# A vision tower on one core: two buffers moved to the front of SBUF, and a new written-out order for every engine

## The chip, the core and the metric

The kernel runs on one core of a Trainium2 chip. Times are device microseconds (us) of one execution. A core has engines that each work through their own list of instructions in order: TensorE (PE; PEld is its weight load), VectorE (DVE), ScalarE (ACT), GpSimd (POOL), and SyncE (SP), which here only issues transfers. Semaphores tie the lists together. 16 DMA engines move data between HBM and the on-chip memory SBUF; TensorE writes to PSUM.

## What is computed

64 images of 12 channels, 224 x 224, pass through one block of a vision transformer. Cut to what matters:

```python
pooled = x.reshape(B, C, 14, 16, 14, 16).sum(axis=(3, 5))         # 16 x 16 patches
h = einsum('bcij,ce->bije', pooled, channel_weights).reshape(B, 196, 192)
h = h + attention(layernorm(h), W_qkv, b_qkv)                     # one head, softmax over 196 keys
h = h + ffn(layernorm(h), w_fc * C0, b_fc * c0b, w_proj * C1, b_proj * c1b)   # tanh GELU, 768 hidden
```

All is float32. The images are 154 MB, the output is 9.6 MB.

## The kernel before, in words

The images are worked through in 16 groups of 4. A group is 3 tiles of 16 image planes; a tile lies in one of the two slots of the ring `xs` (`RING = 2`), with 128 partitions and 7 runs of 896 floats in each. One transfer loads one run of a tile for all partitions (`load`, L403 to L407): 128 rows of 3,584 bytes. SyncE issues the runs of a tile in three chunks of 2, 2 and 3 (`load_chunk`, L409); a chunk waits until VectorE has summed the chunk that lay in the same place two tiles earlier (L414).

VectorE sums each chunk over its patches (`reduce_chunk`, L464, the instruction at L474), nine chunks a group, and does a few small steps of each group between them: `variance1`, `maxima` (L490), `context`, `variance2`.

TensorE takes a group's sums (`sum_rows`, L702) when all nine are there, and then goes through the chain of the attention: `turn_phat`, `apply_a`, `scores` (L730), `turn_maxima`, `turned_scores`, `weigh`, `turn_context`, `turn_u`, `apply_g2`, `turn_uhat` (L796), with ScalarE's copies out of PSUM, VectorE's steps and GpSimd's scalings between them. Then come `hidden` in three pairs, each followed by ScalarE's GELU and rounding to a high part and GpSimd's low part (`low_part`), and `project` in 24 parts of 6 matmuls (L823), on top of `residual`. ScalarE copies the results out of PSUM (`take_out`, L1012, the copy at L1016), and SyncE stores them in two transfers for each group (`send`, L418).

What each engine does next is written out by hand. `PE_ORDER`, `ACT_ORDER`, `DVE_ORDER`, `POOL_ORDER` and `SP_ORDER` (L72 to L200) give for each kind of work one number for each of the 16 groups. Group m's work stands at step `PERIOD * m` plus that number, `PERIOD` being 254, and each engine's list is made by walking through the steps. Only the order that results reaches the chip; what waits for what is in the semaphores. TensorE, for one, works on several groups at a time: behind `sum_rows` of the last group in its list there still stand all 24 parts of `project` of groups 13, 14 and 15, and some of group 12.

Buffers are laid out in SBUF in the order in which they are declared, each start rounded up to 32 bytes. `xs` is declared at L279, behind 25 buffers of constants and weights, and starts at byte 49,952 of each partition. That is 32 bytes past a multiple of 64, and 32 past a multiple of 256. All 14 rows of a partition in it start 32 bytes past a multiple of 64 too, since a row is 56 x 64 bytes. `out_sb` (L296), from which the results are stored in rows of 1,536 bytes, starts at 215,648, also 32 past a multiple of 64.

Of the kernel before, what the change touches and what calls it, by code (L numbers as in the profile page):

```python
# [17 lines left out]
EMBED = 192  # L18
# [9 lines left out]
HALF = TOKENS // 2  # L28
# [9 lines left out]
RUNS = GRID // 2  # L38
RUN = 4 * SIDE
# [31 lines left out]
STEPS = 4907  # L71
PE_ORDER = {  # L72
    "sum_rows": (443, 399, 379, 379, 370, 383, 371, 360, 348, 336, 325, 312, 318, 310, 312, 330),
    "turn_phat": (518, 475, 471, 450, 443, 470, 471, 459, 448, 421, 410, 397, 395, 366, 396, 397),
    "apply_a": (531, 487, 494, 473, 466, 495, 495, 483, 472, 444, 432, 420, 419, 400, 414, 410),
    "scores": (545, 624, 528, 543, 506, 528, 514, 502, 490, 479, 467, 455, 443, 422, 451, 430),
    "turn_maxima": (601, 693, 643, 596, 573, 579, 568, 556, 544, 533, 520, 498, 497, 488, 485, 464),
    "turned_scores": (615, 707, 657, 610, 588, 595, 583, 571, 560, 548, 536, 513, 512, 503, 513, 480),
    "weigh": (644, 739, 695, 646, 619, 631, 619, 608, 596, 584, 572, 544, 543, 549, 559, 516),
    "turn_context": (663, 780, 732, 675, 643, 658, 646, 634, 623, 611, 598, 587, 570, 572, 590, 542),  # L80
    "turn_u": (701, 813, 753, 706, 671, 707, 695, 684, 672, 660, 648, 636, 592, 626, 607, 570),
    "apply_g2": (714, 826, 788, 735, 699, 728, 717, 705, 693, 682, 669, 658, 610, 641, 632, 589),
    "residual": (
        (720, 836, 1053, 1046, 1031, 1019, 1007, 996, 984, 972, 960, 960, 928, 924, 893, 828),
        (970, 1174, 1187, 1157, 1145, 1134, 1122, 1110, 1098, 1086, 1080, 1065, 1032, 1042, 997, 913),
    ),
    "turn_uhat": (763, 882, 835, 808, 765, 802, 790, 779, 767, 738, 732, 726, 685, 714, 693, 635),
    "hidden": (
# [3 lines left out]
    ),  # L92
    "project": (
# [27 lines left out]
    "load_exp": (360, 626, 481, 544, 502, 500, 525, 513, 501, 490, 478, 466, 454, 450, 446, 432),  # L121
    "copy_p_tok": (455, 409, 396, 389, 383, 411, 393, 381, 369, 358, 346, 334, 347, 322, 337, 340),
    "copy_phat": (525, 482, 483, 465, 455, 489, 479, 467, 456, 436, 424, 412, 408, 377, 404, 405),
    "copy_b": (540, 497, 503, 484, 478, 523, 509, 497, 485, 465, 454, 441, 430, 415, 435, 421),
    "copy_maxima": (610, 702, 651, 604, 582, 588, 576, 565, 553, 541, 529, 506, 506, 497, 493, 473),
    "exponentials": (628, 720, 670, 623, 602, 608, 596, 585, 573, 561, 549, 526, 525, 516, 527, 493),
    "load_gelu": (642, 938, 898, 870, 881, 869, 858, 846, 834, 822, 795, 799, 785, 795, 761, 677),
    "copy_context": (657, 752, 716, 664, 632, 649, 638, 626, 614, 603, 590, 560, 560, 563, 574, 532),
    "copy_u": (709, 820, 782, 720, 693, 722, 710, 699, 687, 675, 663, 651, 602, 634, 621, 582),
    "keep_u": (713, 824, 793, 735, 729, 749, 738, 726, 701, 690, 677, 678, 606, 638, 633, 593),  # L130
    "copy_uhat": (770, 889, 842, 815, 790, 810, 798, 786, 775, 747, 740, 733, 694, 723, 701, 656),
    "gelu": (
# [6 lines left out]
    ),  # L139
    "round_high": (  # L140
# [6 lines left out]
    ),  # L147
    "take_out": (
# [4 lines left out]
    ),  # L153
}
DVE_ORDER = {
# [39 lines left out]
    ),  # L195
    "send": (
        (1066, 1272, 1285, 1255, 1244, 1231, 1220, 1208, 1196, 1180, 1176, 1163, 1130, 1140, 1095, 1011),
        (1188, 1405, 1398, 1379, 1367, 1355, 1343, 1332, 1319, 1308, 1312, 1276, 1275, 1243, 1180, 1096),
    ),
}  # L200
SETUP_AT = {
# [954 lines left out]
```

## Time and profile before

| | us |
|---|---|
| runs shown | 493.0, 492.98, 492.1 (median 492.98) |
| the profiled execution | 492.97 |
| its span, first to last instruction | 491.2 |
| TensorE busy | 424.0 (86% of the span) |
| VectorE busy | 381.6 (78%) |
| ScalarE busy | 286.9 (58%) |
| GpSimd busy | 255.5 (52%) |
| DMA share while images are loaded | 1.03 |
| last reduction of the last group ends | 423.7 |
| last matmul ends | 487.5 |

The profile is one execution taken by the hardware profiler. A row of windows gives for a stretch of time how long each engine was busy in it and how many instructions it ran. The chain of waits is followed back from the last instruction: each piece is what released the next. Where rows name a line such as L602, that is a helper which emits every matmul; such rows are told apart by their operands. Matmuls overlap in the pipeline, so their durations add up to more than the busy time; the spacing of their starts is what one costs in a row of them. TensorE's granted clock has two levels, 2.4 and 1.2 GHz; the windows give its mean as a share of the higher.

### The profile page before, as it was taken

How to read it: one execution, taken by the hardware profiler on the slowest of the kernel's cores; microseconds unless marked ns; L12 is line 12 of the kernel's file. 1: busy time of each engine (PE TensorE's matmuls, PEld its weight loads, DVE VectorE, ACT ScalarE, POOL GpSimd, SP SyncE). 2: the span in 40 equal slices, each digit the busy share in tenths (PEclk: the TensorE clock that was granted, in tenths of full speed). 3: DMA queues.
4: the chain of work that ended last, by engine and by line, in shares of the span. 5: the costliest groups of instructions: out<-in, count | busy, mean ns of one | idle time of the engine just before them, and what ended most of it. 6: DMA issues, size and time to landing. Idle time of an engine off the chain costs nothing.

```text
span 491.2 us, 10938 instructions
## 1 busy us (share of the span) xinstructions
PE 424.0 (86%) x4558; PEld 360.5 (73%) x4558; DVE 381.6 (78%) x272; ACT 286.9 (58%) x478; POOL 255.5 (52%) x194
## 2 busy tenths in 40 slices
PE   5966466976989999899998979899999989999996
PEld 4533234864778888688887968887878878888996
DVE  1789998999899998899989898989998887610000
ACT  1022036514877856658585949485858566877821
POOL 1023225503757491738374938375745665576840
PEclk9996555995699999989999999899999989999999
DMA  8999999999999999999999999999999997101101
GB/s 256 360 403 405 401 402 402 402 403 405 402 403 402 404 402 404 400 398 404 397 404 399 400 397 399 400 396 399 402 402 400 397 399 308 34 26 35 41 26 50
DMA packets 56661, 166.65 MB, mean 339 GB/s; under 512 B 5972, under 2 KB 13030, under 8 KB 56612
## 3 DMA queue, kind: packets, MB, share of 16 engines
q1 hardware_dynamic: 56612, 165.95, 87.7%
q8 instruction: 36, 0.59, 0.5%
q14 instruction: 13, 0.11, 0.1%
HBM read 156.29 MB, written 9.63 MB: 338 GB/s over the span
## 4 chain that ended last, share of the span: by engine, by line
DMA 49%; PE 23%; DVE 18%; SPq 5%; issue 3%; ACT 1%; DVEq 0%
DMA xs<-x 49%; PE ps L602 22%; DVE pooled L474 17%; SPq L406 5%; DMA cw_sb<-cw 0%; DVE phat_tok L492 0%; ACT out_sb L1016 0%; PE ps L799 0%; ACT probs L905 0%; DVEq L469 0%; PE ps L779 0%; DVE prod L483 0%; PE ps L786 0%; ACT qkt L903 0%; SPq L425 0%
## 5 line engine op out<-in xcount | busy, mean ns | idle before, releaser
L474 DVE TENSOR_REDUCE pooled<-xs 128x28 f32<-128x1792 f32 x144 | 329.5, 2324 | 29.0 <-DMA xs<-x 28.3
L1114 POOL TENSOR_TENSOR h_lo<-h_f,h_hi 128x784 fp32r<-128x784 f32 x96 | 177.1, 1871 | 76.7 <-ACT h_hi L1010 76.7
L602 PE MATMUL ps<-w_hi,h_hi 128*98 128x192 f32 x768 | 207.1, 270 | 1.1 <-POOL h_lo L1114 1.0
L602 PE MATMUL ps<-w_lo,h_hi 128*98 128x192 f32 x768 | 196.5, 256 | 0.0
L602 PE MATMUL ps<-w_hi,h_lo 128*98 128x192 f32 x768 | 196.2, 255 | 0.0
L602 PEld LDWEIGHTS ps<-w_hi,h_hi 128*98 128x98 f32 x768 | 128.4, 167 | 16.7 <-issue 14.5
L602 PEld LDWEIGHTS ps<-w_lo,h_hi 128*98 128x98 f32 x768 | 128.9, 168 | 0.0
L602 PEld LDWEIGHTS ps<-w_hi,h_lo 128*98 128x98 f32 x768 | 128.5, 167 | 0.0
L1001 ACT ACTIVATE h_f<-ps 128x784 f32<-128x784 f32 x96 | 75.8, 827 | 21.4 <-PE ps L602 20.4
L1010 ACT CAST h_hi<-h_f 128x784 fp32r<-128x784 f32 x96 | 78.4, 855 | 0.0
L1091 POOL TENSOR_TENSOR inv<-var,minus_half 98x8 f32<-98x8 f32 x16 | 26.2, 1640 | 77.4 <-DVE var L488 77.4
L602 PE MATMUL ps<-rows_sb,f_rows 32*128 32x196 f32 x768 | 50.6, 382 | 6.0 <-ACT h_f L1001 3.7
L1016 ACT COPY out_sb<-ps 98x384 f32<-98x384 f32 x64 | 30.2, 477 | 30.8 <-PE ps L602 30.6
L602 PEld LDWEIGHTS ps<-rows_sb,f_rows 32*128 32x128 f32 x768 | 34.6, 203 | 15.3 <-issue 5.9
L1105 POOL TENSOR_TENSOR inv<-var,minus_half 98x8 f32<-98x8 f32 x16 | 26.2, 1640 | 28.2 <-DVE var L513 28.2
L960 ACT ACTIVATE probs<-ps 98x1568 f32<-98x1568 f32 x16 | 23.7, 1481 | 23.5 <-PE ps L602 23.5
L492 DVE TENSOR_REDUCE phat_tok<-ps 98x8 f32<-98x1568 f32 x16 | 28.5, 1784 | 6.5 <-PE ps L602 6.5
L602 PE MATMUL ps<-rows_sb 32*98 32x196 f32 x512 | 31.6, 363 | 1.8 <-ACT rows_sb L953 1.2
L602 PE MATMUL ps<-resid,rows_sb 32*98 32x192 f32 x256 | 27.9, 336 | 2.5 <-ACT out_sb L1016 2.5
L953 ACT COPY rows_sb<-ps 128x196 f32<-128x196 f32 x16 | 5.2, 323 | 36.8 <-PE ps L756 36.7
L602 PEld LDWEIGHTS ps<-rows_sb 32*98 32x98 f32 x512 | 20.4, 169 | 6.4 <-ACT rows_sb L953 2.0
L602 PEld LDWEIGHTS ps<-resid,rows_sb 32*98 32x98 f32 x256 | 20.1, 163 | 5.3 <-ACT out_sb L1016 3.7
(119 smaller groups left out, 340.2 us busy)
## 6 DMA issues: line engine op xcount, KB each, us to landing
xs<-x SPq DMA_DIRECT2D x336, 448.0 KB, 12.5
out<-out_sb SPq DMA_DIRECT2D x32, 294.0 KB
rows_sb<-wfc SPq DMA_DIRECT2D x1, 576.0 KB, 5.7
out_sb<-wproj SPq DMA_DIRECT2D x1, 576.0 KB, 9.4
h_f<-wqkv SPq DMA_DIRECT2D x1, 432.0 KB
cf<-const_full SPq DMA_DIRECT2D x1, 264.0 KB, 2.8
h_f<-const_paired SPq DMA_DIRECT2D x1, 153.0 KB, 3.3
cr<-const_rows SPq DMA_DIRECT2D x1, 83.2 KB
```

The costliest lines, as they stand in the source:

```text
L406: sp.dma_start(xs[:, tile % RING, i], x_runs[2 * PLANES * tile:2 * PLANES * (tile + 1), :, i]).then_inc(x_landed[tile % RING][i], 16)
L474: dve.tensor_reduce(pooled[:, n % 2, t, GRID * first:GRID * end].rearrange("p (i j) -> p i j", j=GRID), runs, AX.XY, ALU.add).then_inc(red ...
L492: dve.tensor_reduce(phat_tok[:, m % 2, :, :, NEG].rearrange("p h b -> p b h"), ps[0:HALF, 0:GROUP, 0:2 * TOKENS].rearrange("p b (h k) -> p ...
L602: return pe.matmul(o, a, b, start=start, stop=stop, skip_group_check=shared)
L953: act.copy(phat_neg, ps[:, MB, 0:TOKENS]).then_inc(phat_neg_ready, 1)
L960: act.activation(probs[:], ps[0:HALF, 0:GROUP, 0:2 * TOKENS], ACT.Exp).then_inc(probs_ready, 1)
L1001: act.activation(h_f32[:, t].rearrange("p (b n) -> p b n", b=GROUP), ps[:, 0:GROUP, TOKENS * (t % 2):TOKENS * (t % 2 + 1)], ACT.Gelu_apprx ...
L1010: act.copy(h_hi[:, m % 2, t], h_f32[:, t]).then_inc(h_hi_ready, 1)
L1016: act.copy(out_sb[:, b // 2, b % 2], ps[0:HALF, OB + b % 2, 0:2 * EMBED]).then_inc(out_ready, 1)
L1091: pool.tensor_tensor(inv1[:], var1[:], minus_half[:], ALU.pow).then_inc(inv1_ready, 1)
L1105: pool.tensor_tensor(inv2[:], var2[:], minus_half[:], ALU.pow).then_inc(inv2_ready, 1)
L1114: pool.tensor_tensor(h_lo[:, m % 2, t], h_f32[:, t], h_hi[:, m % 2, t].bitcast(F32), ALU.subtract).then_inc(h_lo_ready, 1)
```

## The change

`xs` and `out_sb` are declared first of all buffers. `xs` then starts at byte 16,512 (258 x 64, and 128 past a multiple of 256), `out_sb` at 66,688 (1,042 x 64, and 128 past a multiple of 256). Every other buffer moves by a multiple of 256 bytes (by 56,320 those ahead of `xs` before, by 6,144 those behind it), so its place within 64 or 256 bytes stays. All five tables are replaced; the work itself, its tiles, semaphores and waits stay as they are. Of the tables the diff below shows the rows of which the next sections speak; the columns are groups 0 to 15.

```diff
-STEPS = 4907
+STEPS = 4901
 PE_ORDER = {
-    "sum_rows": (443, 399, 379, 379, 370, 383, 371, 360, 348, 336, 325, 312, 318, 310, 312, 330),
+    "sum_rows": (443, 399, 379, 361, 374, 370, 363, 346, 339, 330, 316, 307, 298, 293, 287, 275),
...
-    "turn_context": (663, 780, 732, 675, 643, 658, 646, 634, 623, 611, 598, 587, 570, 572, 590, 542),
+    "turn_context": (663, 766, 694, 657, 658, 687, 669, 653, 644, 639, 630, 621, 602, 555, 527, 516),
...
     "residual": (
-        (720, 836, 1053, 1046, 1031, 1019, 1007, 996, 984, 972, 960, 960, 928, 924, 893, 828),
-        (970, 1174, 1187, 1157, 1145, 1134, 1122, 1110, 1098, 1086, 1080, 1065, 1032, 1042, 997, 913),
+        (720, 824, 1046, 1034, 1009, 991, 975, 966, 961, 953, 944, 940, 918, 910, 867, 802),
+        (970, 1171, 1173, 1149, 1132, 1093, 1083, 1093, 1084, 1066, 1046, 1054, 1043, 1015, 971, 887),
     ),
...
     "project": (
-        (857, 1025, 1065, 1066, 1051, 1039, 1027, 1016, 1007, 995, 983, 969, 937, 933, 902, 854),
-        (894, 1063, 1086, 1055, 1040, 1028, 1017, 1005, 996, 981, 969, 974, 948, 967, 933, 837),
-        (931, 1127, 1116, 1097, 1100, 1088, 1077, 1051, 1038, 1035, 1029, 1020, 1000, 1002, 964, 875),
-        (868, 1046, 1122, 1071, 1060, 1048, 1036, 1024, 1012, 1000, 989, 985, 942, 956, 913, 859),
-        (899, 1073, 1111, 1092, 1080, 1069, 1057, 1045, 1033, 1030, 1009, 1006, 976, 997, 949, 864),
-        (937, 1138, 1153, 1117, 1105, 1094, 1082, 1070, 1058, 1046, 1035, 1031, 1005, 1013, 970, 886),
-        (873, 1036, 1070, 1082, 1070, 1059, 1047, 1035, 1023, 1016, 999, 1000, 971, 951, 907, 870),
-        (910, 1079, 1105, 1060, 1045, 1034, 1022, 1010, 1001, 990, 974, 980, 987, 982, 944, 843),
-        (942, 1143, 1158, 1123, 1111, 1099, 1087, 1076, 1063, 1060, 1040, 1036, 1011, 1007, 975, 881),
-        (862, 1031, 1076, 1112, 1086, 1074, 1062, 1065, 1053, 1041, 1015, 1026, 982, 961, 918, 891),
-        (905, 1068, 1091, 1077, 1065, 1053, 1042, 1030, 1017, 1010, 994, 991, 953, 977, 938, 848),
-        (952, 1149, 1164, 1128, 1116, 1105, 1093, 1081, 1069, 1066, 1045, 1042, 1016, 1018, 981, 897),
-        (1012, 1208, 1221, 1168, 1156, 1144, 1133, 1121, 1109, 1097, 1089, 1082, 1042, 1081, 1017, 933),
-        (982, 1258, 1262, 1193, 1182, 1170, 1158, 1147, 1134, 1122, 1123, 1107, 1123, 1092, 1023, 939),
-        (1029, 1263, 1268, 1210, 1198, 1186, 1174, 1163, 1150, 1139, 1142, 1124, 1129, 1102, 1028, 966),
-        (1007, 1252, 1226, 1204, 1192, 1181, 1169, 1157, 1145, 1133, 1137, 1118, 1118, 1107, 1012, 960),
-        (988, 1190, 1251, 1179, 1167, 1155, 1144, 1132, 1119, 1108, 1104, 1102, 1109, 1052, 1039, 922),
-        (1045, 1277, 1276, 1241, 1229, 1217, 1211, 1199, 1187, 1170, 1168, 1138, 1134, 1123, 1060, 971),
-        (1023, 1217, 1235, 1246, 1234, 1223, 1216, 1205, 1192, 1175, 1173, 1143, 1076, 1113, 1050, 949),
-        (1051, 1185, 1202, 1173, 1162, 1150, 1138, 1126, 1114, 1102, 1095, 1097, 1081, 1063, 1006, 944),
-        (1061, 1222, 1246, 1252, 1240, 1228, 1222, 1210, 1198, 1186, 1179, 1153, 1087, 1118, 1055, 955),
-        (1018, 1247, 1241, 1199, 1187, 1175, 1164, 1152, 1140, 1128, 1131, 1113, 1047, 1058, 1033, 976),
-        (1056, 1283, 1197, 1228, 1216, 1204, 1196, 1184, 1172, 1160, 1157, 1129, 1062, 1087, 1044, 928),
-        (1070, 1288, 1282, 1262, 1251, 1239, 1227, 1216, 1203, 1191, 1196, 1162, 1153, 1129, 1066, 982),
+        (857, 1021, 1060, 1049, 1031, 1014, 984, 975, 984, 963, 967, 954, 939, 919, 876, 816),
+        (894, 1060, 1055, 1043, 1026, 1009, 995, 986, 978, 973, 953, 949, 944, 930, 892, 811),
+        (931, 1120, 1101, 1089, 1072, 1055, 1046, 1041, 1030, 1025, 1014, 1009, 995, 965, 938, 827),
+        (868, 1038, 1066, 1068, 1051, 1030, 1015, 1006, 1000, 993, 984, 974, 950, 924, 881, 860),
+        (899, 1076, 1071, 1074, 1056, 1036, 1020, 1011, 1005, 999, 989, 979, 970, 981, 912, 843),
+        (946, 1125, 1106, 1094, 1077, 1061, 1052, 1047, 1035, 1030, 1019, 1014, 1006, 987, 944, 865),
+        (873, 1032, 1081, 1063, 1042, 1025, 1010, 1000, 994, 988, 978, 969, 990, 945, 923, 822),
+        (910, 1065, 1117, 1109, 1092, 1050, 1035, 1025, 1019, 1013, 1003, 995, 976, 960, 917, 849),
+        (937, 1131, 1146, 1114, 1097, 1071, 1061, 1061, 1050, 1040, 1025, 1020, 1001, 976, 949, 854),
+        (862, 1027, 1086, 1054, 1037, 1020, 990, 981, 989, 968, 973, 960, 960, 970, 887, 833),
+        (905, 1070, 1111, 1079, 1062, 1045, 1026, 1017, 1014, 1004, 998, 989, 955, 940, 907, 838),
+        (952, 1151, 1151, 1120, 1102, 1076, 1067, 1067, 1055, 1045, 1030, 1025, 1020, 992, 954, 870),
+        (979, 1198, 1217, 1158, 1141, 1107, 1098, 1110, 1101, 1075, 1061, 1065, 1066, 1031, 1007, 896),
+        (1033, 1227, 1211, 1169, 1152, 1127, 1118, 1121, 1112, 1095, 1090, 1076, 1088, 1070, 1012, 939),
+        (1038, 1264, 1241, 1184, 1167, 1141, 1132, 1136, 1127, 1109, 1095, 1081, 1094, 1086, 1023, 945),
+        (1015, 1233, 1182, 1189, 1172, 1156, 1146, 1141, 1132, 1124, 1112, 1099, 1060, 1037, 996, 901),
+        (1028, 1253, 1193, 1164, 1146, 1122, 1112, 1116, 1107, 1090, 1084, 1071, 1055, 1051, 1018, 918),
+        (1044, 1269, 1257, 1197, 1180, 1163, 1154, 1149, 1140, 1135, 1117, 1105, 1135, 1097, 1029, 950),
+        (984, 1180, 1188, 1234, 1217, 1201, 1192, 1187, 1174, 1169, 1165, 1143, 1104, 1026, 980, 928),
+        (990, 1238, 1226, 1226, 1208, 1192, 1183, 1178, 1165, 1161, 1159, 1135, 1099, 1075, 991, 912),
+        (1022, 1258, 1235, 1240, 1223, 1206, 1197, 1192, 1180, 1175, 1170, 1149, 1124, 1092, 1034, 934),
+        (1009, 1211, 1262, 1220, 1203, 1178, 1168, 1172, 1160, 1146, 1131, 1116, 1119, 1042, 1002, 907),
+        (1004, 1216, 1246, 1202, 1185, 1169, 1159, 1154, 1145, 1140, 1126, 1110, 1141, 1081, 985, 923),
+        (1058, 1274, 1268, 1245, 1228, 1212, 1203, 1197, 1188, 1180, 1175, 1154, 1146, 1102, 1039, 955),
     ),
...
 DVE_ORDER = {
     "reduce": (
-        (101, 162, 140, 114, 123, 114, 105, 96, 87, 78, 69, 60, 55, 53, 54, 55),
+        (100, 162, 140, 114, 123, 114, 105, 96, 87, 78, 69, 60, 51, 42, 33, 24),
...
-        (387, 365, 338, 347, 338, 329, 320, 311, 302, 293, 285, 279, 278, 279, 280, 297),
+        (387, 365, 338, 329, 338, 329, 320, 311, 302, 293, 285, 276, 267, 258, 249, 240),
     ),
...
 SP_ORDER = {
     "load": (
-        (98, 110, 103, 94, 73, 64, 60, 51, 42, 33, 24, 15, 10, 1, 0, 8),
+        (118, 130, 123, 114, 93, 84, 80, 71, 57, 48, 44, 35, 21, 12, 3, 0),
...
     ),
     "send": (
-        (1066, 1272, 1285, 1255, 1244, 1231, 1220, 1208, 1196, 1180, 1176, 1163, 1130, 1140, 1095, 1011),
-        (1188, 1405, 1398, 1379, 1367, 1355, 1343, 1332, 1319, 1308, 1312, 1276, 1275, 1243, 1180, 1096),
+        (1086, 1289, 1291, 1267, 1250, 1211, 1201, 1205, 1193, 1180, 1164, 1172, 1156, 1126, 1089, 1005),
+        (1196, 1418, 1406, 1381, 1363, 1347, 1337, 1333, 1324, 1316, 1312, 1290, 1282, 1237, 1174, 1090),
     ),
...
...
             return ctx.enter_context(nc.semaphore(name))
 
 
+        xs = sb("xs", [128, RING, RUNS, RUN])
+        out_sb = sb("out_sb", [HALF, 2, 2, 2 * EMBED])
+
+
         cf = sb("cf", [128, FULL])
         cr = sb("cr", [CHANNELS, ROWS])
         cw_sb = sb("cw_sb", [CHANNELS, EMBED])
...
         table_out = sb("table_out", [1, 1])
 
 
-        xs = sb("xs", [128, RING, RUNS, RUN])
         pooled = sb("pooled", [128, 2, TILES, HALF])
         u_tok = sb("u_tok", [HALF, 2, 2, GROUP, Q])
         prod1 = sb("prod1", [HALF, 2 * GROUP, CHANNELS + 1])
...
         h_f32 = sb("h_f32", [128, H_SLOTS, GROUP_TOKENS])
         h_hi = sb("h_hi", [128, 2, HT, GROUP_TOKENS], F32R)
         h_lo = sb("h_lo", [128, 2, HT, GROUP_TOKENS], F32R)
-        out_sb = sb("out_sb", [HALF, 2, 2, 2 * EMBED])
 
         phat_rows, phat_neg, b_rows, context_rows, u_rows, uhat_rows = (rows_sb[:, i] for i in range(6))
         u_kept = [rows_sb[:, 6], rows_sb[:, 7]]
```

## Rows read from the trace of the kernel before

**Rows 1.** The page: busy time by engine, and moved GB/s in 40 equal slices.

```profile
...
PE 424.0 (86%) x4558; PEld 360.5 (73%) x4558; DVE 381.6 (78%) x272; ACT 286.9 (58%) x478; POOL 255.5 (52%) x194
...
GB/s 256 360 403 405 401 402 402 402 403 405 402 403 402 404 402 404 400 398 404 397 404 399 400 397 399 400 396 399 402 402 400 397 399 308 34 26 35 41 26 50
```

**Rows 2.** The page: chain that ended last, shares by line.

```profile
...
DMA xs<-x 49%; PE ps L602 22%; DVE pooled L474 17%; SPq L406 5%; DMA cw_sb<-cw 0%; DVE phat_tok L492 0%; ACT out_sb L1016 0%; PE ps L799 0%; ACT probs L905 0%; DVEq L469 0%; PE ps L779 0%; DVE prod L483 0%; PE ps L786 0%; ACT qkt L903 0%; SPq L425 0%
```

**Rows 3.** Chain from 396 us on: start us, length us, what ran.

```profile
...
453.70 17.70 PE ps L602 x208
...
480.02 7.53 PE ps L602 x80
```

**Rows 4.** Windows: length, busy us (and count) per engine, granted clock, DMA share, GB/s.

```profile
...
core 0: us, PE busy (x) PEld busy (x) DVE busy (x) ACT busy (x) POOL busy (x), PEclk, DMA share, GB/s
162.70:423.70 261.00, 242.19 (x2879) 213.95 (x2878) 235.72 (x160) 180.11 (x299) 152.72 (x111) 0.98 1.00 388
423.70:487.60 63.90, 62.28 (x728) 56.27 (x726) 4.65 (x12) 37.88 (x64) 39.21 (x25) 1.00 0.10 30
36.00:162.70 126.70, 93.86 (x867) 72.20 (x868) 119.86 (x80) 62.14 (x104) 58.65 (x42) 0.73 1.03 403
```

**Rows 5.** Timeline of VectorE about the last reductions of groups 5 and 15: start, length.

```profile
...
157.83 4.87 DVE L474 TENSOR_REDUCE pooled<-xs 128x28 f32<-128x1792 f32 x2
...
414.08 9.66 DVE L474 TENSOR_REDUCE pooled<-xs 128x42 f32<-128x2688 f32 x4
```

**Rows 6.** Waits, 162.7 to 423.7 us, VectorE's (and SyncE's queue, 95 to 406).

```profile
...
DVE pooled L474 <- DMA xs<-x: 21.0, 27, 1.7
DVE phat_tok L492 <- PE ps L602: 2.1, 1, 2.1
...
SPq L406 <- DVE pooled L474: 89.5, 64, 3.4
SPq L420 <- ACT out_sb L1016: 3.0, 4, 2.1
```

**Rows 7.** VectorE's instructions by form, whole span: busy us, mean ns, idle before.

```profile
...
L474 DVE TENSOR_REDUCE pooled<-xs 128x28 f32<-128x1792 f32 x96 | 190.6, 2011 | 3.7 <-DMA xs<-x 3.3
L474 DVE TENSOR_REDUCE pooled<-xs 128x42 f32<-128x2688 f32 x48 | 141.6, 2950 | 25.3 <-DMA xs<-x 24.9
```

**Rows 8.** TensorE's waits, 162.7 to 423.7 us: total, times, longest.

```profile
...
PE ps L799 <- POOL uhat_tok L1107: 11.0, 7, 3.3
PE ps L602 <- DVE pooled L474: 3.1, 3, 1.5
```

**Rows 9.** Windows by rate, columns as in group 4.

```profile
...
12.00:15.00 3.00, 3.00 (x16) 3.00 (x15) 2.77 (x2) 0.02 (x1) 0.00 (x0) 1.00 1.03 408
...
162.70:406.00 243.30, 224.49 (x2662) 198.65 (x2661) 220.12 (x152) 167.11 (x278) 146.25 (x106) 0.98 1.03 400
```

**Rows 10.** Timeline of TensorE: one residual and three matmuls of a project part.

```profile
...
408.24 0.89 PE L602 MATMUL ps<-resid,rows_sb 32*98 32x192 f32 x8
409.06 0.33 PE L602 MATMUL ps<-w_hi,h_hi 128*98 128x192 f32 x1
409.23 0.25 PE L602 MATMUL ps<-w_lo,h_hi 128*98 128x192 f32 x1
409.32 0.25 PE L602 MATMUL ps<-w_hi,h_lo 128*98 128x192 f32 x1
409.41 0.26 PE L602 MATMUL ps<-w_hi,h_hi 128*98 128x192 f32 x1
```

**Rows 11.** The page: transfers, KB of one, us from issue to landing.

```profile
...
xs<-x SPq DMA_DIRECT2D x336, 448.0 KB, 12.5
out<-out_sb SPq DMA_DIRECT2D x32, 294.0 KB
```

**Rows 12.** Timeline at the end: last copy out of PSUM, issue of last store.

```profile
...
487.57 0.48 ACT L1016 COPY out_sb<-ps 98x384 f32<-98x384 f32 x1 [0.58 <-PE ps L602]
488.07 0.32 SPq L420 DMA_DIRECT2D out<-out_sb  x1
```

More of the change, by code:

```diff
@@ L70 @@
 PERIOD = 254
-STEPS = 4907
+STEPS = 4901
 PE_ORDER = {
-    "sum_rows": (443, 399, 379, 379, 370, 383, 371, 360, 348, 336, 325, 312, 318, 310, 312, 330),
[L74 to L79, printed above, removed]
-    "turn_context": (663, 780, 732, 675, 643, 658, 646, 634, 623, 611, 598, 587, 570, 572, 590, 542),
-    "turn_u": (701, 813, 753, 706, 671, 707, 695, 684, 672, 660, 648, 636, 592, 626, 607, 570),
-    "apply_g2": (714, 826, 788, 735, 699, 728, 717, 705, 693, 682, 669, 658, 610, 641, 632, 589),
+    "sum_rows": (443, 399, 379, 361, 374, 370, 363, 346, 339, 330, 316, 307, 298, 293, 287, 275),
+    "turn_phat": (518, 475, 458, 449, 441, 470, 455, 438, 412, 403, 407, 423, 370, 361, 378, 323),
+    "apply_a": (531, 487, 541, 471, 460, 489, 493, 476, 462, 453, 445, 440, 424, 388, 400, 368),
+    "scores": (545, 624, 556, 537, 518, 511, 509, 492, 493, 483, 461, 471, 450, 419, 422, 389),
+    "turn_maxima": (601, 688, 633, 589, 568, 576, 559, 558, 549, 529, 518, 527, 501, 477, 458, 427),
+    "turned_scores": (615, 703, 646, 603, 584, 592, 575, 574, 564, 544, 533, 543, 527, 492, 473, 443),
+    "weigh": (644, 741, 676, 634, 629, 632, 615, 624, 615, 594, 585, 593, 567, 523, 504, 489),
+    "turn_context": (663, 766, 694, 657, 658, 687, 669, 653, 644, 639, 630, 621, 602, 555, 527, 516),
+    "turn_u": (701, 801, 733, 677, 691, 723, 706, 690, 680, 675, 663, 658, 629, 588, 544, 540),
+    "apply_g2": (714, 819, 750, 699, 714, 743, 725, 709, 700, 695, 690, 685, 647, 622, 563, 558),
@@ L83 @@
     "residual": (
-        (720, 836, 1053, 1046, 1031, 1019, 1007, 996, 984, 972, 960, 960, 928, 924, 893, 828),
-        (970, 1174, 1187, 1157, 1145, 1134, 1122, 1110, 1098, 1086, 1080, 1065, 1032, 1042, 997, 913),
+        (720, 824, 1046, 1034, 1009, 991, 975, 966, 961, 953, 944, 940, 918, 910, 867, 802),
+        (970, 1171, 1173, 1149, 1132, 1093, 1083, 1093, 1084, 1066, 1046, 1054, 1043, 1015, 971, 887),
     ),
-    "turn_uhat": (763, 882, 835, 808, 765, 802, 790, 779, 767, 738, 732, 726, 685, 714, 693, 635),
+    "turn_uhat": (763, 864, 828, 781, 805, 794, 787, 777, 768, 757, 755, 740, 711, 672, 652, 609),
@@ L120 @@
 ACT_ORDER = {
[L121 to L131, printed above, removed]
-    "gelu": (
[6 rows of a table removed]
+    "load_exp": (360, 626, 480, 535, 511, 488, 507, 490, 481, 472, 459, 447, 445, 430, 419, 413),
+    "copy_p_tok": (455, 409, 396, 371, 391, 417, 385, 368, 362, 353, 338, 326, 331, 316, 301, 285),
+    "copy_phat": (525, 482, 477, 460, 451, 480, 471, 454, 457, 447, 423, 434, 414, 378, 395, 359),
+    "copy_b": (540, 497, 551, 488, 476, 503, 504, 487, 478, 469, 456, 462, 434, 398, 416, 379),
+    "copy_maxima": (610, 697, 641, 598, 577, 585, 568, 567, 558, 538, 526, 536, 510, 485, 466, 436),
+    "exponentials": (628, 716, 660, 616, 597, 605, 588, 587, 577, 557, 546, 556, 541, 505, 486, 456),
+    "load_gelu": (642, 928, 884, 865, 873, 856, 855, 846, 831, 819, 824, 809, 774, 755, 724, 643),
+    "copy_context": (657, 754, 689, 648, 647, 649, 632, 643, 633, 610, 599, 612, 588, 544, 520, 502),
+    "copy_u": (709, 808, 745, 686, 706, 737, 719, 699, 690, 689, 684, 680, 640, 608, 558, 547),
+    "keep_u": (713, 812, 820, 717, 737, 753, 735, 727, 717, 705, 696, 714, 699, 644, 569, 551),
+    "copy_uhat": (770, 871, 836, 790, 813, 801, 795, 785, 776, 764, 763, 748, 719, 696, 662, 621),
+    "gelu": (
[6 rows of a table added]
     ),
     "round_high": (
[6 rows of a table removed]
[6 rows of a table added]
     ),
     "take_out": (
[4 rows of a table removed]
[4 rows of a table added]
     ),
@@ L156 @@
     "reduce": (
[9 rows of a table removed]
-    ),
-    "variance1": (486, 435, 426, 417, 408, 434, 425, 416, 407, 363, 354, 349, 353, 334, 349, 347),
-    "maxima": (581, 662, 556, 574, 545, 556, 527, 518, 509, 501, 495, 474, 475, 436, 464, 443),
-    "context": (694, 804, 746, 697, 653, 673, 664, 656, 652, 647, 608, 601, 582, 609, 596, 549),
-    "variance2": (729, 848, 801, 772, 713, 754, 745, 736, 727, 692, 684, 685, 643, 651, 640, 598),
[9 rows of a table added]
+    ),
+    "variance1": (486, 435, 426, 417, 408, 434, 390, 381, 372, 363, 354, 375, 336, 327, 324, 290),
+    "maxima": (581, 662, 613, 554, 545, 536, 527, 518, 509, 501, 492, 503, 474, 445, 436, 403),
+    "context": (694, 784, 726, 667, 682, 699, 690, 661, 652, 663, 654, 645, 616, 572, 533, 522),
+    "variance2": (729, 830, 781, 722, 733, 754, 745, 736, 727, 718, 709, 700, 662, 633, 572, 566),
 }
 POOL_ORDER = {
-    "scale_p": (493, 442, 433, 424, 415, 441, 444, 432, 421, 371, 362, 356, 367, 341, 368, 370),
-    "scale_u": (738, 857, 810, 781, 736, 776, 765, 753, 740, 713, 707, 700, 655, 682, 666, 607),
+    "scale_p": (493, 442, 433, 424, 415, 444, 397, 389, 380, 371, 362, 395, 344, 335, 351, 297),
+    "scale_u": (738, 839, 804, 748, 776, 767, 758, 749, 740, 731, 727, 713, 686, 646, 611, 576),
     "low_part": (
[6 rows of a table removed]
[6 rows of a table added]
     ),
```

80 rows, old and new, of tables (ACT_ORDER, DVE_ORDER, PE_ORDER, POOL_ORDER) are left out of this document.

## Prediction

> **What bounds the kernel now.** I read the page first. TensorE is busy for 86% of the span and VectorE for 78%, and the moved GB/s stand at 396 to 405 from the third slice of the span to the thirty-third and drop to some 30 behind it [rows 1]. So there are two stretches with different limits: images arrive until about 420 us, and then something runs for 70 us without them. The chain of waits says the same: 49% of the span is images landing, 17% VectorE's sums over them, 5% SyncE issuing the next load, and 22% TensorE [rows 2], and from 396 us on nearly every long piece is TensorE [rows 3].
>
> Next I cut the span where the images end. The last reduction of group 5 ends at 157.83 + 4.87 = 162.7 us, that of group 15 at 414.08 + 9.66 = 423.7 us [rows 5]. That is 261.0 us for ten groups, 26.1 us a group. In this stretch VectorE is busy for 235.7 us, TensorE for 242.2, and the DMA share is 1.00, 1.03 until the loads run out [rows 4, 9]. All three are near full. Which ends last is seen in the waits: VectorE sat idle before 27 reductions for 21.0 us until images landed, and only 3.0 us until TensorE was done [rows 6]. So the images set the pace, but by little: without the wait for them VectorE would need 240 us for the ten groups (24.0 a group), and TensorE's busy time is 24.2 a group. Over the whole span VectorE waits 28.2 us for images [rows 7].
>
> Behind 423.7 us TensorE is busy for 62.3 of 63.9 us [rows 4]: this stretch is the work that stands in TensorE's list behind the last group's `sum_rows`, and it starts when that group's images are summed. Then follow the last copy at 487.57 us, the last store's issue at 488.07 [rows 12], and its landing. Profiled, the execution took 492.97 us, 1.8 more than the span and practically the median of the runs (492.98); I make the sum against 492.97.
>
> **Part 1, the buffers' places.** It removes and adds no instruction. What it can change is the time of one row's landing. A group brings 21 transfers of 448 KB and two stores of 294 KB [rows 11], 10.24 MB; at the 400 GB/s of the stretch [rows 9] that is 25.6 us of the 26.1. With the engines' share at 1.03 there is no gap to close, so a faster group needs faster rows. No row of this trace shows a row of images landing at another offset, so I bound the group's time. The slow end is 26.1 us, if the place makes no difference. I set no loss: each row keeps its length and its 3,584 bytes, the source stays, and the start only goes from 32 past a multiple of 64 to a multiple. The fast end is set by the engines behind the loads: VectorE's 24.0 and TensorE's 24.2. The highest rate that a window shows is 408 GB/s [rows 9], in the first images, before VectorE had work for more than one chunk; 400/408 of 26.1 would be 25.6, but that rate was reached at the old place, and says nothing of the new. Nothing here lies nearer to one end than to the other, so I take the middle of 24.0 and 26.1, 25.05 us. Ten groups then end at 162.7 + 250.5 = 413.2 us: **10.5 us earlier**.
>
> The page "DMA: Bandwidth & Descriptors" of the Trainium skill, section "Where 436 GB/s comes from", puts the ceiling of the 16 ports at 435 GB/s; as an estimate, 400/435 of 26.1 is 24.0 us a group, so the ceiling would not bind ahead of the two engines. The same page, section "How a descriptor splits into AXI transactions", speaks against the change: what costs is a start off a multiple of 256 bytes on the side that is read. That side is HBM here and does not move, and 16,512 is off 256 too; by this rule the images would land no faster, which is the first rival below.
>
> Before 162.7 us the images' share of VectorE's waits is 28.2 - 21.0 = 7.2 us, and TensorE is far from full there: 93.9 of 126.7 us at a mean granted clock of 0.73 [rows 4]. Work there hangs on latencies and on setup, so I count nothing, with a bound of 3 us gained. `out_sb`'s new place touches 32 stores, of which only the last is on the path, issue to landing about 3 us: nothing, with a bound of 0.3 either way.
>
> **Part 2, the new orders.** Of TensorE's list I count what stands behind the last group's `sum_rows`, as that work cannot start before group 15's images are summed. Steps behind 254 x 15 + 330 = 4140 before, 4085 after: groups 13 to 15 have all 24 project parts there in both. Of group 12 (254 x 12 = 3048) it is the parts later than 1092 before, 6 of them, and those later than 1037 after, 12 of them. So six parts more. Matmuls of a part start 0.09 us apart [rows 10]; 6 x 6 x 0.09 = 3.2 us. The second `residual` of group 12 (1043) also falls behind now, 0.8 us [rows 10], and `turn_context` of group 14 (527) moves ahead, two matmuls, 0.2 us. Sum +3.8 us. TensorE's idle of 63.9 - 62.3 = 1.6 us could take up part of it, so 2.2 to 3.8; I take **+3.0 us**. If the images come no faster, nothing covers it. These parts are taken out of the time before `sum_rows`, where TensorE must have room: it idles 18.8 us in 162.7 to 423.7, of which 11.0 is `turn_uhat` waiting for GpSimd and 3.1 the wait for reductions [rows 8]. The first hangs on `variance2`, which stands in VectorE's list behind reductions that wait for images, so these waits shrink with them. 10.5 - 3.0 = 7.5 us of the 18.8 have to go; that leaves more than 1 us a group for latencies.
>
> VectorE's, ScalarE's and GpSimd's lists hold the same instructions. SyncE's loads move 2 us later against its stores. A store that waits for `out_ready` holds up the loads behind it; in 95 to 406 us this cost 3.0 us of SyncE's time in four waits, against 89.5 us of waiting for reductions [rows 6], and a load is issued 12.5 us before it lands [rows 11], so such a wait is covered. Nothing, with a bound of 1 us lost: the cover goes if a store waits longer than those 12.5 us.
>
> **Sum.** 492.97 - 10.5 + 3.0 = 485.5 us. The end follows group 15's images one for one, since TensorE is full behind them.
>
> **Rivals.** First, the place makes no difference. Then the group stays at 26.1 us, the last images are summed at 423.7 as before, and six more parts and a residual stand behind them: 492.97 + 2.2 to 3.8 = 495.2 to 496.8, or from 493.5 if the earlier stages that the new order puts ahead shorten the path too. For it: nothing in the trace shows an effect of the place. By the rule of the Trainium skill above it is the case to expect. Against it: with engines at 1.03 and a steady 403 GB/s [rows 4], the pace is that of one row, which is what the place could touch. This is the slower side, and its price decides it: images must end over 3.0 us earlier, that is below 25.8 us a group, or the new order loses.
>
> Second, a small effect, 25.5 to 25.8 us a group: images 3 to 6 us earlier, the order 3 us later, 490 to 493.
>
> Third, images come as fast as the engines take them. At 24.5 us a group, the last are summed 16 us earlier, and 3.0 us of it go back: 480. TensorE would have to lose 13 of its 18.8 us idle, which the wait for GpSimd alone hardly allows; with 10 to 13 gained, 480 to 483.
>
> Fourth, TensorE's list waits where it did not before, since it was laid out for other arrival times: `project` parts late, a store held up, `out_sb` not free. Some 2 to 4 us on the forecast, 488 to 490, or on the first rival, 497 to 499.
>
> **Chances.** My forecast with its own range, 483 to 489 us: 0.45. Engines take over, 480 to 483: 0.13. Small effect, 489 to 493.5: 0.13, of which 0.05 lies within 0.2% (1.0 us, about what a measurement of this kernel can tell from no change). No effect of the place, 493.5 to 496.8: 0.25, of which 0.03 within 0.2%. A badly fitting order, slower: 0.04. So faster 0.45 + 0.13 + 0.08 = 0.66, same 0.08, slower 0.26. The range goes from 481, which leaves out 0.05 below, to 496, which leaves out about 0.12 above.
>
> **What would show it.** Right: 415 to 420 GB/s in the slices in which now 400 stand; VectorE's wait for images well under 21 us; the last reduction ending at 410 to 416 us; about 67 us from there to the last copy (63.9 now), with TensorE full. Wrong: slices at 400 and a last reduction at 423 (first rival), VectorE's reductions back to back with a DMA share under 1 (third), or TensorE idle behind the last reduction (fourth).

## The result, and the profile after

The changed kernel takes 489.63 us (median), the kernel before 492.99 beside it: ratio 0.9927, 95% interval 0.9905 to 0.9948, 3.4 us less. The forecast was 485.5, 7.5 us less. The direction was right and the time lies in the range, but only 3.4 us of the 7.5 came. The profiled execution took 489.43 us over a span of 487.6.

The moved GB/s of the changed kernel in 40 slices, and its chain of waits by line (of [rows 1] and [rows 2]):

```profile
...
GB/s 245 345 406 407 405 406 404 406 408 409 406 406 407 408 409 406 410 403 407 408 404 406 410 404 406 407 405 407 405 407 407 406 404 273 28 26 40 37 26 51
...
```

```profile
...
DMA xs<-x 48%; PE ps L604 21%; DVE pooled L476 18%; SPq L408 4%; DVE phat_tok L494 1%; DMA cw_sb<-cw 0%; POOL h_lo L1116 0%; POOL inv L1107 0%; ACT out_sb L1018 0%; PE ps L781 0%; DVE prod L485 0%; PE ps L758 0%; ACT probs L907 0%; DVE var L490 0%; PE ps L801 0%
...
```

The slices stand at 403 to 410, where 396 to 405 stood. I had asked for 415 to 420. The chain has the same shape as before. Next the windows, cut where the last reductions of groups 5 and 15 end (of [rows 4]):

```profile
...
core 0: us, PE busy (x) PEld busy (x) DVE busy (x) ACT busy (x) POOL busy (x), PEclk, DMA share, GB/s
163.80:416.70 252.90, 236.21 (x2824) 206.02 (x2824) 234.93 (x161) 177.04 (x295) 152.41 (x110) 0.99 1.00 397
416.70:484.10 67.40, 66.14 (x776) 59.99 (x768) 4.71 (x11) 41.42 (x67) 39.43 (x25) 1.00 0.11 33
...
```

VectorE's timeline of the changed kernel about these two reductions (start and length in us, line, operation and tiles; of [rows 5]):

```profile
...
158.95 4.87 DVE L476 TENSOR_REDUCE pooled<-xs 128x28 f32<-128x1792 f32 x2
...
408.05 1.78 DVE L494 TENSOR_REDUCE phat_tok<-ps 98x8 f32<-98x1568 f32 x1
409.75 6.91 DVE L476 TENSOR_REDUCE pooled<-xs 128x28 f32<-128x1792 f32 x3
...
```

Group 5 ends at 158.95 + 4.87 = 163.8 us, 1.1 us later than before. Group 15 ends at 409.75 + 6.91 = 416.7 us, 7.0 us earlier. In between a group takes 25.3 us (26.1 before). The window from 416.7 us to just behind the start of the last copy out of PSUM (484.0) has 67.4 us (63.9 before), with TensorE busy for 66.1 of it and 776 matmuls in place of 728. So images end 7.0 us earlier, and 3.5 us of that are given back behind them; the other half is the gain.

VectorE's waits of the changed kernel in the first of these windows (us in total, times, longest; of [rows 6]):

```profile
...
DVE pooled L476 <- DMA xs<-x: 16.0, 18, 1.9
...
```

TensorE's in the same window (of [rows 8]):

```profile
...
PE ps L801 <- POOL uhat_tok L1109: 6.4, 7, 2.3
PE ps L604 <- DVE pooled L476: 6.0, 8, 1.2
...
```

VectorE still waits 16.0 us for images (21.0 before), and TensorE's wait for GpSimd's `uhat_tok` fell from 11.0 to 6.4 us. The images still set the pace; they only set a slightly faster one.

### The profile page after: what moved, and what is told of

Read it like the earlier page. It is cut to its first block, busy times and chain, and to the rows that moved or that the text cites. A ratio compares the mean times of both kernels' runs of the same rounds, so it can differ in the third digit from the quotient of the medians.

```text
span 487.6 us, 10938 instructions
## 1 busy us (share of the span) xinstructions
PE 426.1 (87%) x4558; PEld 359.6 (74%) x4558; DVE 380.3 (78%) x272; ACT 287.5 (59%) x478; POOL 255.3 (52%) x194
## 4 chain that ended last, share of the span: by engine, by line
DMA 48%; PE 22%; DVE 20%; SPq 5%; issue 3%; ACT 1%; POOL 1%; DVEq 0%
DMA xs<-x 48%; PE ps L604 21%; DVE pooled L476 18%; SPq L408 4%; DVE phat_tok L494 1%; DMA cw_sb<-cw 0%; POOL h_lo L1116 0%; POOL inv L1107 0%; ACT out_sb L1018 0%; PE ps L781 0%; DVE prod L485 0%; PE ps L758 0%; ACT probs L907 0%; DVE var L490 0%; PE ps L801 0%
## 5 line engine op out<-in xcount | busy, mean ns | idle before, releaser
L1003 ACT ACTIVATE h_f<-ps 128x784 f32<-128x784 f32 x96 | 75.7, 827 | 22.9 <-PE ps L604 22.6
L1012 ACT CAST h_hi<-h_f 128x784 fp32r<-128x784 f32 x96 | 79.8, 854 | 0.0
L494 DVE TENSOR_REDUCE phat_tok<-ps 98x8 f32<-98x1568 f32 x16 | 28.5, 1784 | 9.4 <-PE ps L604 9.4
L992 ACT COPY rows_sb<-ps 128x196 f32<-128x196 f32 x16 | 8.4, 522 | 34.5 <-PE ps L801 34.5
```

Of the source, the lines that this page charges most:

```text
L494: dve.tensor_reduce(phat_tok[:, m % 2, :, :, NEG].rearrange("p h b -> p b h"), ps[0:HALF, 0:GROUP, 0:2 * TOKENS].rearrange("p b (h k) -> p ...
L992: act.copy(uhat_rows.rearrange("p (h n) -> p n h", h=2), ps[:, MB, 0:TOKENS].rearrange("p (n h) -> p n h", h=2)).then_inc(uhat_rows_ready, 1)
L1003: act.activation(h_f32[:, t].rearrange("p (b n) -> p b n", b=GROUP), ps[:, 0:GROUP, TOKENS * (t % 2):TOKENS * (t % 2 + 1)], ACT.Gelu_apprx ...
L1012: act.copy(h_hi[:, m % 2, t], h_f32[:, t]).then_inc(h_hi_ready, 1)
```

## The experiments

The theory: the images' rows land faster at the new place, and the new order costs time behind the last image. The rival: the place does nothing, and the pace comes from the order in which SyncE issues transfers. A further question: why the gain in rate was so small.

### Each part alone

The tables of before with the new places:

```diff
 (after)
-PE_ORDER, ACT_ORDER, DVE_ORDER, POOL_ORDER, SP_ORDER, STEPS of after
+those of before
```

> The five tables of before, xs and out_sb declared first. Theory 1 (the place makes the images' rows land faster, the new order costs time behind the last image): 405 to 407 GB/s while images load, about 25.3 us a group, the last reduction ends at 416 to 418 us, 63.9 us from there to the last copy as before, time 485.5 to 487.5. Rival (the place does nothing, the images' pace comes from the order in which SyncE issues loads and stores): 400 to 403 GB/s, last reduction at 423 to 424, 492 to 494.

The tables of after with the old places:

```diff
 (before)
-PE_ORDER, ACT_ORDER, DVE_ORDER, POOL_ORDER, SP_ORDER, STEPS of before
+those of after
```

> The five tables of after, xs and out_sb declared where they stood before. Theory 1: 400 to 403 GB/s, 26.1 us a group, last reduction at 423 to 425 us, 67.3 us from there to the last copy, time 495 to 498. Rival (order alone): 406 GB/s, last reduction at 417, time 489 to 490.

Windows of the first (columns as in the windows above): its rates are those of after.

```profile
...
24.00:60.00 36.00, 19.59 (x77) 11.74 (x76) 32.08 (x20) 7.36 (x16) 11.53 (x6) 0.69 1.03 406
165.00:400.00 235.00, 219.10 (x2598) 194.09 (x2597) 216.55 (x150) 163.75 (x272) 142.54 (x102) 0.98 1.03 406
...
```

Windows of the second: its rates are those of before.

```profile
...
24.00:60.00 36.00, 21.00 (x77) 12.65 (x75) 32.14 (x20) 7.36 (x15) 11.54 (x6) 0.80 1.03 403
165.00:400.00 235.00, 215.61 (x2564) 188.29 (x2563) 214.18 (x146) 161.85 (x268) 138.73 (x100) 0.99 1.03 400
...
```

Place alone: 487.89 us, ratio 0.9893 (0.9863 to 0.9922). Order alone: 495.04 us, ratio 1.0042 (1.0020 to 1.0063). The rival falls, since the rate follows the place. The whole gain is the place's. Yet the place alone gave less than I had expected of it before the run: its last reduction ends at 419.6 us where 416 to 418 were expected, at the expected rate of 406 GB/s. The order costs 2 us at the old place, and at the new one the median is 1.7 us above that of the place alone (there the two intervals still overlap a little). In one table, from the profiled executions, one for each kernel (group pace and stretches from VectorE's timeline and the last copy's start); such an execution can lie a microsecond off its kernel's median, as that of e1_place_only does (488.93 us):

| kernel | tables | `xs` past a multiple of 256 | GB/s, 24 to 60 / 165 to 400 us | group 5 ends | us a group, 5 to 15 | group 15 ends | from there to last copy |
|---|---|---|---|---|---|---|---|
| before | before | 32 | 403 / 400 | 162.7 | 26.1 | 423.7 | 63.9 |
| e2_order_only | after | 32 | 403 / 400 | 163.9 | 25.8 | 422.1 | 67.9 |
| e1_place_only | before | 128 | 406 / 406 | 162.1 | 25.75 | 419.6 | 63.8 |
| after | after | 128 | 406 / 406 | 163.8 | 25.3 | 416.7 | 67.3 |
| e5_256_old_order | before | 0 | 417 / 411 | 161.9 | 25.2 | 413.5 | 63.8 |
| e3_xs_256 | after | 0 | 417 / 411 | 160.8 | 24.95 | 410.3 | 67.1 |

The last column shows the order's cost: 3.3 to 4.0 us at each place. The column before it shows a gain of the order that I had not counted: group 15 ends 1.6 to 3.2 us earlier with the new tables. VectorE's timeline in e1_place_only shows from where:

```profile
...
408.27 1.79 DVE L494 TENSOR_REDUCE phat_tok<-ps 98x8 f32<-98x1568 f32 x1 [2.09 <-PE ps L604]
409.97 9.66 DVE L476 TENSOR_REDUCE pooled<-xs 128x42 f32<-128x2688 f32 x4
```

With the old tables VectorE stands idle for 2.09 us before `maxima` (L494) of group 14, because TensorE's `scores` are not there, and four reductions of group 15 stand behind it. In after the same `maxima` at 408.05 has no wait ahead of it and three reductions follow (the timeline above). Over the ten groups VectorE's waits for TensorE in e1_place_only (162.1 to 419.6 us) are these two lines:

```profile
...
DVE phat_tok L494 <- PE ps L604: 4.1, 2, 2.1
DVE prod L510 <- PE ps L604: 2.1, 2, 1.5
...
```

That is 6.2 us, against 0.5 in after (2.9 in before, none in e2_order_only). So part of the pace of after is the order's: images at 406 GB/s with the old tables gave 25.75 us a group.

### Another place for the images, and for the output

```diff
 (after)
+        sb("pad", [128, 32])           # 128 bytes: xs and out_sb at multiples of 256
         xs = sb("xs", [128, RING, RUNS, RUN])
         out_sb = sb("out_sb", [HALF, 2, 2, 2 * EMBED])
+        sb("pad2", [128, 32])
```

> As after, with 128 bytes of padding ahead of xs, so that xs and out_sb start at a multiple of 256 (a further 128 bytes behind them keep the other buffers' places). If 64 bytes are what counts: as after, 406 GB/s with images alone, 407 with stores beside them, time 489 to 490.5. If the pieces of a row are cut at multiples of 256 bytes on the landing side too, a row has 14 pieces in place of 15: rate up once more, 410 to 415 GB/s, last reduction at 411 to 414 us, time 484 to 487.

Windows of e3_xs_256, and VectorE's wait for images in it (160 to 410.4 us):

```profile
...
24.00:60.00 36.00, 22.01 (x89) 13.45 (x91) 33.14 (x20) 7.68 (x16) 11.54 (x6) 0.81 1.03 417
165.00:400.00 235.00, 221.61 (x2645) 193.92 (x2637) 220.51 (x154) 167.13 (x277) 147.59 (x108) 0.99 1.03 411
...
```

```profile
...
DVE pooled L478 <- DMA xs<-x: 13.3, 16, 2.1
...
```

482.62 us, ratio 0.9780 (0.9749 to 0.9811): 417 GB/s with images alone, 411 with stores beside them, 24.95 us a group. The rate and the time are better than either branch expected. It is about the pace that I had forecast for the change (25.05), 128 bytes further on; the images end at 410.3, within the forecast's 410 to 416. One row of 3,584 bytes takes a DMA engine 140.1 ns on average between 24 and 60 us here, 144.1 in after and 145.4 in before (from the DMA packets in the traces), so the rows themselves are faster, as the prediction had it. The other starts have the same edit with other sizes of `pad`, 192, 224 and 384 bytes, and a `pad2` that keeps all other buffers in place:

> As after, with 192 bytes ahead of xs: it starts 64 past a multiple of 256 (other buffers keep their places). If a multiple of 64 gives the first step and a multiple of 256 the second: 405 to 406 GB/s at 24 to 60 us, time 489 to 490. If a multiple of 128 is what gave after its 406: 403 GB/s, 495 to 497.

> The kernel of e6_xs_64, timed in rounds. If 64 past 256 is a step worse than 128 once stores run (403.5 against 406.3 GB/s in the one look): 491 to 493.5, 2 to 3 us above after's 489.6. If that look was an outlier: 489 to 490.5.

> As after, with xs (and out_sb) at 96 past a multiple of 256, so 32 past one of 64. If what counts first is a multiple of 64: 403 GB/s at 24 to 60 us and 400 with stores, as with 32 past 256, time 494 to 497. If any start that leaves a longer first piece up to the next 256 is as good as 64 or 128: 405 to 406, 489 to 493.

> As after, with 384 bytes ahead of xs: it starts at a multiple of 512 (e3_xs_256: 256 past one). If 256 is the last step: as e3, 417 GB/s at 24 to 60 us, 482 to 483. If there is a further step at 512: 420 or more, 480 to 482.

Windows at 64 past a multiple of 256 (e11), at 96 (e9), and of after, at 128:

```profile
...
24.00:60.00 36.00, 20.64 (x75) 12.43 (x73) 31.70 (x24) 7.36 (x15) 11.53 (x6) 0.83 1.03 406
165.00:400.00 235.00, 216.41 (x2572) 188.08 (x2571) 216.05 (x150) 163.21 (x271) 139.05 (x101) 0.99 1.03 403
...
```

```profile
...
24.00:60.00 36.00, 20.80 (x77) 12.64 (x75) 31.48 (x20) 7.45 (x15) 11.53 (x6) 0.81 1.03 406
165.00:400.00 235.00, 220.03 (x2608) 192.54 (x2607) 216.91 (x151) 163.46 (x272) 142.38 (x102) 0.99 1.03 405
...
```

```profile
...
24.00:60.00 36.00, 20.62 (x75) 12.40 (x73) 30.86 (x19) 7.35 (x15) 11.53 (x6) 0.81 1.03 406
165.00:400.00 235.00, 219.60 (x2622) 192.00 (x2625) 217.37 (x151) 164.45 (x273) 143.08 (x105) 0.99 1.03 406
...
```

| `xs` past a multiple of 256, tables of after | GB/s, 24 to 60 / 165 to 400 us | us | ratio to before |
|---|---|---|---|
| 32 (e2, `xs` at its old place) | 403 / 400 | 495.04 | 1.0042 (1.0020 to 1.0063) |
| 64 (e11; e6, timed once) | 406 / 403; 406 / 404 | 492.76; 492.79 | 0.9997 (0.9980 to 1.0015) |
| 96 (e9) | 406 / 405 | 490.8 | 0.9966 (0.9951 to 0.9981) |
| 128 (after) | 406 / 406 | 489.63 | 0.9927 (0.9905 to 0.9948) |
| 0, 256 past 512 (e3) | 417 / 411 | 482.62 | 0.9780 (0.9749 to 0.9811) |
| 0, also of 512 (e7, timed once) | 417 / 411 | 482.56 | |

So 64 bytes are not what counts. A start 32 past a multiple of 64 (96) does better than a multiple of 64 (64), whose 492.8 us lay in neither of the ranges expected of e6. Of the starts tried only the multiples of 256 give the large step, and 512 adds nothing to it. Among the other starts the rate with stores rises from 32 to 128, that is with the shorter of the two end pieces of a row (a row of 14 x 256 bytes that starts 32 past a multiple leaves 224 bytes up to the next one and 32 at its end). That this is the cause isn't shown: starts above 128, which would tell it from the start itself, weren't tried.

One rival is left for the step from before to after. In e2 `xs` lies at byte 49,952, in all the others of this table between 16,512 and 16,896, and no kernel had it at the front and 32 past a multiple of 256. So the step from 403 to 406 GB/s with images alone may come of the 32 bytes or of the move to the front; no run tells these apart. The step from 406 to 417 is free of this, since after and e3_xs_256 differ by 128 bytes alone.

The output's place alone, 32 past a multiple of 64 again beside images at 128 (e4), and at 160 past 256 beside images at 256 (e10):

```diff
 (after; for e10 with the pad of e3 ahead of xs)
         xs = sb("xs", [128, RING, RUNS, RUN])
+        sb("pad", [128, 8])            # e10: 40
         out_sb = sb("out_sb", [HALF, 2, 2, 2 * EMBED])
+        sb("pad2", [128, 56])
```

> As after, with out_sb alone 32 bytes past a multiple of 64 again (padding ahead of it and behind it; all other places kept). If the images' place is all that counts: 406 to 407 GB/s, last reduction at 416 to 418, time 489 to 490.5. If the stores' place is what lets images through while stores run (400 against 407 GB/s there, only 403 against 406 before the first store): 402 to 404 GB/s from 160 us on, last reduction at 419 to 421, time 492 to 494.

> As e3_xs_256, with out_sb alone at 160 past a multiple of 256. If only the images' place counts: 417 and 411 GB/s as in e3, 482 to 483.5. If the stores' rows gain from a multiple of 256 too: 406 to 409 with stores, 484 to 487.

489.33 us (after: 489.63) and 482.73 us (e3: 482.62): the output's place does nothing, as far as 0.1% can be told. Nor does it touch the stores' own rows: one of 1,536 bytes takes a DMA engine 65.1 to 65.2 ns on average between 165 and 400 us in all four (from the DMA packets in the traces).

### The old order at the best place

The tables of before with the padding of e3:

> The tables of before, with xs and out_sb at multiples of 256 as in e3_xs_256. If the two parts add: the loads as in e3 (417 GB/s with images alone, 411 with stores), 63.8 us from the last reduction to the last copy in place of 67, and the last reduction 2 to 3 us later than in e3 since VectorE's old order puts a wait for TensorE ahead of it: 481 to 483. If the new order only pays once the images come at this rate (its arrival times were made for it): 484 to 486, TensorE idle between 160 and 410 us as in before.

482.91 us, ratio 0.9784 (0.9742 to 0.9826), against 482.62 with the new tables. The order costs nothing here: 3.3 us less behind the last reduction, and that reduction 3.2 us later (the table of parts). So the tables laid out anew pay off at none of the three places where both sets were run, and do no harm where images come at 417 GB/s. Of all kernels run with full work, e3_xs_256 and its equals e5, e7 and e10 are the fastest, 7 us under the changed kernel.

### Images no limit at all

```diff
 (after)
-    sp.dma_start(xs[:, tile % RING, i], x_runs[2 * PLANES * tile:2 * PLANES * (tile + 1), :, i]).then_inc(...)
+    w = RUN if tile < RING else RUN // 2
+    sp.dma_start(xs[:, tile % RING, i, 0:w], x_runs[2 * PLANES * tile:2 * PLANES * (tile + 1), :, i, 0:w]).then_inc(...)
```

> As after, but from the third tile on only the first half of each row of the images is loaded (the other half keeps older data, so the sums are of other pixels). It prices the case in which images are no limit. If the engines behind take over at 24.0 to 24.5 us a group: VectorE waits under 3 us for images, last reduction ends at 402 to 408 us, 66 to 67 us more to the last copy, time 475 to 481. If the lists' order holds the engines to the pace of after whatever the images do: last reduction at 413 to 417, 487 to 490.

467.08 us (timed once), less than either branch expected. Its windows:

```profile
...
159.60:394.10 234.50, 231.85 (x2817) 203.74 (x2820) 232.94 (x161) 175.86 (x295) 152.15 (x110) 1.00 0.72 223
394.10:461.80 67.70, 66.39 (x784) 60.20 (x776) 4.70 (x11) 41.66 (x68) 39.42 (x25) 1.00 0.11 33
...
```

Its waits of VectorE in the first window:

```profile
...
DVE prod L511 <- PE ps L605: 0.3, 1, 0.3
DVE pooled L477 <- issue: 0.2, 1, 0.2
```

And those of TensorE, whose wait for `uhat_tok` is 0.5 us (11.0 before [rows 8]):

```profile
...
PE ps L605 <- DVE pooled L477: 1.6, 3, 0.6
PE ps L802 <- POOL uhat_tok L1110: 0.5, 1, 0.5
...
```

VectorE waits for no image, and a group takes 23.4 us. Both engines are full, VectorE for 232.9 of 234.5 us and TensorE for 231.9. VectorE waits 0.5 us in all, while TensorE still waits 1.6 us for VectorE's sums, so VectorE sets the pace, with TensorE close behind it. The tail is 67.7 us, as in after (67.4). The end of the program follows the last reduction: against after that comes 22.6 us earlier and the last copy 22.4.

## Why the prediction went wrong

**What bounds the kernel, and that its end follows the images: right.** In after, e1, e2, e3 and e8 the end moves with group 15's last reduction, and what lies behind depends only on the tables, 63.8 to 63.9 us with the old and 67.1 to 67.9 with the new.

**The step that failed: part 1, the group's pace, 25.05 us as the middle of 24.0 and 26.1, and with it the 10.5 us.** The place alone gave 25.75 us a group (e1_place_only); its last images are summed 4.1 us earlier, and its median is 5.3 us lower. The 25.3 of after are the place and the order together. By rate it is plainer: I needed some 415 GB/s, and the place 128 past a multiple of 256 gives 406. The middle was a choice between two ends with nothing to decide by. What could have cast doubt on it stood in the text: that 16,512 is off 256 too. I read the rule of the Trainium skill ("DMA: Bandwidth & Descriptors", "How a descriptor splits into AXI transactions") as one for the side that is read, HBM here, and put it into the first rival as a case of no effect. e3 and e7 show that a multiple of 256 counts on the landing side as well. The rule's count of beats doesn't rank the other starts, though: carried over to the landing side, as an estimate, it would make 32 the cheapest of them and 128 the dearest, and with stores beside them the runs show the reverse.

**Before 162.7 us: counted at nothing, cost 1.1 us.** I set a bound on the gain side alone. The new tables put group 3's `maxima` where TensorE's `scores` are not ready. In after VectorE waits 1.87 us there, with group 4's reductions behind it (its timeline, the wait in brackets):

```profile
...
133.87 1.79 DVE L494 TENSOR_REDUCE phat_tok<-ps 98x8 f32<-98x1568 f32 x1 [1.87 <-PE ps L604]
...
```

In e2's timeline of VectorE the same wait is 1.30 us:

```profile
...
133.94 1.79 DVE L492 TENSOR_REDUCE phat_tok<-ps 98x8 f32<-98x1568 f32 x1 [1.30 <-PE ps L602]
...
```

In before and e1 there is none in that place, and in these two group 5 ends at 162.7 and 162.1, against 163.8 and 163.9. In e3 the wait is there too (1.84 us), but its images gain more ahead of it, and group 5 ends at 160.8. Together with the ten groups, 252.9 - 250.5 + 1.1 = 3.5 us: this is what images fell short of the 10.5 us. With 0.5 us more behind them than the 3.0 forecast, that makes 4.0 us, which is 485.5 against the 489.43 of the profiled execution.

**The order's +3.0 us (2.2 to 3.8): right in the count, incomplete in the sum.** Six parts of `project` and a `residual` more stand behind `sum_rows`, 44 matmuls; the window counts 776 for 728, and the stretch grew by 3.5 us in after and 4.0 in e2. What I left out is that VectorE's table moved too: no wait of 2 us ahead of the last reductions. By the medians the net cost is 1.7 to 2.0 us with images at 403 to 406 GB/s and nothing at 417.

**The other terms.** The output's place: nothing, as counted (e4, e10). SyncE's shifted loads weren't tried by themselves; its stores wait for results for 6.8 us in after between 95 and 406 us (3.0 before), 3.1 us at the longest, well under the 12.5 us of cover that the prediction counted on. TensorE had the room to be fuller: idle of 16.7 us of 252.9 in after.

**The rivals.** The first, no effect of the place, was priced at 493.5 to 496.8, and e2, which is that case, took 495.0. The second, a small effect, came closest to what happened: 489.63 lies in its 489 to 493.5, and I gave it 0.13. The third I mis-sized: with images no limit I set 480 to 483, since TensorE's waits for GpSimd would hardly go away. e8 took 467.1, at 23.4 us a group, under the 24.0 that I had set as the fast end, and TensorE idles for 2.6 us in ten groups. So those waits were the images' doing; that they came about through `variance2` in VectorE's list, as the prediction had it, fits but was not tried by itself.

## What to carry to other kernels

Put a buffer into which long rows stream at a multiple of 256 bytes, with a row length that keeps every row there (2.2% of this kernel's time, with rows of 3,584 bytes; other lengths weren't tried); check where the allocator put it, since small buffers declared ahead shift it unseen. When a change is said to work through an address, compare the new address with every boundary in question, and not only with the one it is named for. A term that is set at the middle of its bounds for want of a row deserves its own run first, and an order written out by hand is weighed on all engines' lists, not on the fullest one alone.

## What was not expected of the hardware

A transfer of 128 rows of 3,584 bytes that lands at a multiple of 256 bytes in each partition runs at 417 to 418 GB/s, at the other starts tried at 403 to 406 (all 16 DMA engines busy in each case, share 1.03). With stores beside it the spread is 411 to 400. The start of the rows that stores read in SBUF showed no effect (160 or 128 past a multiple of 256 in e4 and after, 160 or 0 in e10 and e3). I had not expected waits between engines that looked like latencies, 11.0 us of TensorE waiting for GpSimd [rows 8], to vanish when images are no limit. Open is why the starts other than 0 differ among themselves, and whether the move to the front of SBUF has a share in the first step.
